# One transformer block on each of eight cores: an earlier first stage, biases as one tile, the last units by tokens

## The reference, cut

```python
xn = layernorm(x)                              # over 1024 channels
q, k, v = split(xn @ W_attn + b_attn)          # 16 heads of 64
att = (q @ k^T) / 8 / temperature + slope_h * (key - query)   # causal
y = softmax(att) @ v @ W_proj + b_proj
h = silu(xn @ (w_gate/127).T) * (xn @ (w_up/127).T)           # 3072 wide
out = x + y + h @ (w_down/127).T
```

## Time and profile before

| what | us |
|---|---|
| median of 3 runs, slowest core | 1230.04 (1229.83 to 1230.42) |
| the profiled execution, device time | 1233.72 |
| its span on core 0, the slowest | 1232.2 |
| spans of the other seven cores | 1224.6 to 1229.4 |
| TensorE busy | 1139.7 (92%) |
| VectorE / ScalarE / GpSimd busy | 588.8 / 528.7 / 239.5 |
| chain that ended last: TensorE's share | 84% |

### The profile page before, as it was taken

One profiled execution on the slowest core, in us unless ns is written; L12 is line 12 of the kernel. 1 busy time (PEld: TensorE's weight loads), 2 busy tenths in 40 slices (PEclk: granted clock), 3 DMA queues, 4 the chain that ended last, 5 costly groups with the idle time before them and its releaser, 6 DMA issues.

```text
span 1232.2 us, 24735 instructions; the slowest of 8 cores (1224.6 to 1232.2 us)
## 1 busy us (share of the span) xinstructions
PE 1139.7 (92%) x7874; PEld 574.5 (47%) x7874; DVE 588.8 (48%) x1194; ACT 528.7 (43%) x963; POOL 239.5 (19%) x292
## 2 busy tenths in 40 slices
PE   2899899999999999999999999999899689999996
PEld 1333345555555555555555555555454234444442
DVE  4442476666666666676566666667661100100000
ACT  0343335665666565565565655556575100000000
POOL 9000112222212222222222112122123300000000
PEclk9999899999999999999999999999999989999998
DMA  8229004322222332132312102122322441424220
GB/s 191 69 87 192 18 28 83 69 62 47 59 58 65 66 66 58 40 69 63 65 36 52 42 23 57 31 52 65 113 53 95 136 163 69 171 98 171 74 69 34
DMA packets 39724, 94.20 MB, mean 76 GB/s; under 512 B 5824, under 2 KB 26433, under 8 KB 38770
## 3 DMA queue, kind: packets, MB, share of 16 engines
q0 software_dynamic: 10352, 44.05, 16.9%
q1 hardware_dynamic: 28768, 48.45, 12.4%
q10 hardware_dynamic: 482, 0.12, 0.0%
HBM read 90.50 MB, written 27.26 MB: 96 GB/s over the span
## 4 chain that ended last, share of the span: by engine, by line
PE 84%; DVE 7%; issue 4%; POOL 2%; DMA 1%; ACT 1%; DVEq 0%; POOLq 0%; ACTq 0%; SPq 0%
PE ps_gu L701 24%; PE ps_dn L866 14%; PE ps_s L790 9%; PE ps_t L771 9%; PE ps_m L682 8%; PE ps_y L806 5%; PE ps_t L733 5%; PE ps_dn L853 4%; DVE cm L544 4%; DMA hb<-h_sc 1%; PE ps_m L819 1%; PE ps_t L775 1%; PE ps_s L793 1%; PE ps_t L737 1%; PE ps_dn L858 1%
## 5 line engine op out<-in xcount | busy, mean ns | idle before, releaser
L544 DVE TENSOR_REDUCE cm<-ps_s 128x1 f32<-128x512 f32 (+3 forms) x640 | 381.4, 608 | 223.9 <-PE ps_s L790 123.4
L650 ACT ACTIVATE pt<-ps_t 128x512 bf16<-128x512 f32 (+1 forms) x576 | 327.6, 576 | 214.3 <-PE ps_t L771 147.4
L701 PE MATMUL ps_gu<-xnT,wubuf 128*128 128x512 bf16 x768 | 264.0, 382 | 2.1 <-DVE hst L472 1.8
L701 PE MATMUL ps_gu<-xnT,wgbuf 128*128 128x512 bf16 x768 | 261.5, 380 | 1.2 <-ACT kst L593 1.2
L790 PE MATMUL ps_s<-kx,qx 67*128 67x512 bf16 (+3 forms) x640 | 219.3, 351 | 29.1 <-DVE cm L544 28.7
L771 PE MATMUL ps_t<-qx,kx 98*128 98x512 bf16 (+3 forms) x640 | 217.1, 349 | 0.6 <-ACT pt L650 0.6
L417 POOL TENSOR_SCALAR th_s<-th_s 128x512 f32<-128x512 f32 x96 | 59.3, 618 | 662.5 <-ACT th_s L601 662.5
L866 PE MATMUL ps_dn<-wdres,hb 128*128 128x512 bf16 x768 | 170.8, 383 | 13.9 <-DMA hb<-h_sc 13.9
L806 PEld LDWEIGHTS ps_y<-Vt,pt 128*128 128x128 bf16 x2176 | 126.5, 97 | 92.5 <-issue 1.3
L806 PE MATMUL ps_y<-Vt,pt 128*128 128x65 bf16 x2176 | 139.8, 193 | 0.0
L582 DVE SCALAR_TENSOR_TENSOR outsb<-ps_dn,xres 128x512 f32<-128x512 f32 x32 | 20.6, 686 | 226.9 <-PE ps_dn L866 226.9
(11 more groups left out here) (76 smaller groups left out, 799.7 us busy)
## 6 DMA issues: line engine op xcount, KB each, us to landing
h_sc<-hst SPq DMA_DIRECT2D x96, 128.0 KB, 1.7
hb<-h_sc SPq DMA_DIRECT2D x4, 3072.0 KB, 13.9
xstage<-xin SPq DMA_DIRECT2D x16, 512.0 KB, 4.7
xres<-xin POOLq DMA_DIRECT2D x16, 512.0 KB, 4.7
out<-outsb POOLq DMA_DIRECT2D x16, 512.0 KB, 3.0
wgbuf<-wg_r POOLq DMA_DIRECT2D x12, 512.0 KB, 6.9
wubuf<-wu_r POOLq DMA_DIRECT2D x12, 512.0 KB, 9.2
wd_sc<-wd_r POOLq DMA_DIRECT2D x12, 512.0 KB, 9.2
```

The costliest lines, as they stand in the source:

```text
L544: e.tensor_reduce(cm[:, c0:c0 + 1], ps_s[:, s % 2 * 512:s % 2 * 512 + w], AX.X, AluOpType.max, negate=True).then_inc(sem["v_mx"], 1)
L650: e.activation(pt[t % NPT][:, 0:w], ps_t[:, t % 2 * 512:t % 2 * 512 + w], AF.Exp).then_inc(sem["a_e"], 1)
L701: mm = e.matmul(ps_gu[:, r // 8 * 512:r // 8 * 512 + 512], w[:, w0:w0 + 128], xnT[:, dc * T + tb * 512:dc * T + tb * 512 + 512], start=(dc ...
```

## The change

- **First stage.** VectorE starts on x without waiting for constants: only TensorE waits for the identity (`l_id`), and VectorE waits for the other four (`l_const`) at i = 1, between tile 0's and tile 1's work. The matmul for the temperature moves to i = 3. GpSimd holds the weights back until the first two x tiles have landed, then issues the first half of the V weights, `wqk_b`, and the second half. V is made of the first column half alone for tiles 0 to 3 (`v_at`); then come q and k of block 0, then the second column half for tiles 0 to 3; from tile 4 on both halves follow each other.
- **Biases.** The rows L737 and L858, `onesb_s`, `bpj_b` and VectorE's work on them are gone. Since the weights of a softmax sum to one, the bias of V reaches the output as `b_v @ W_proj + b_proj`, the same for all tokens. TensorE makes this once before the output stage, in all 128 rows (16 matmuls of bf16 with `bv_b` broadcast and 2 of f32), ScalarE copies it to `bias_b`, and GpSimd adds it to each `xres` tile.
- **Last units by tokens.** Unit f >= 88 takes channels 22 and 23 of token block 0, then of block 1, and so on (`gu_of`). SyncE loads `hb0` after the store of unit 89.
- **Output.** ScalarE issues the stores of `out`; of the last tile the first half is finished before the second is begun, and each is stored alone.

```diff
+            return (f // 4, f % 4) if f < NF_ATT else (f // 8 * 2 + f % 2, f % 8 // 2)
...
+        v_at = {i: [(i - 1, 0)] for i in range(1, 5)}
+        v_at[4] += [(tt, 1) for tt in range(4)]
+        for i in range(5, NT + 1):
+            v_at[i] = [(i - 1, 0), (i - 1, 1)]
...
@@ block.sync
             for f in range(NF_ATT, NF):
                 store_h(f)
-            for tb in range(NTB):
+                if f == NF_ATT + 1:
+                    e.wait_ge(sem["s_h0"], 16 * HCN)
+                    e.wait_ge(sem["p_av"], len(tg))
+                    e.wait_ge(sem["p_yt"], 4 * NHP)
+                    e.dma_start(out=hb0[:, :], in_=h_sc[0, :, :]).then_inc(sem["l_hb0"], 16)
+                    e.dma_start(out=bpj_f[:, :], in_=bproj[:, :]).then_inc(sem["l_bp"], 16)
+            for tb in range(1, NTB):
@@ block.gpsimd
-            for d in range(4):
-                e.dma_start(out=wv_b[:, d * 2048:(d + 1) * 2048],
-                            in_=wv_r[:, d * 2048:(d + 1) * 2048]).then_inc(sem["l_wv"], 16)
-            cast_qk(0)
...
+            e.wait_ge(sem["l_x0"], 16)
+            e.wait_ge(sem["l_x1"], 16)
+            for half in range(2):
+                e.dma_start(out=wv_b[:, half * 4096:(half + 1) * 4096], in_=wv_r[half, :, :]).then_inc(
+                    sem[f"l_wv{half}"], 16)
+                if half == 0:
+                    cast_qk(0)
...
+                if tt >= 2:
+                    e.wait_ge(sem["v_out"], 2 * (tt - 1))
+                    e.dma_start(out=xres[tt % 2][:, :], in_=xin[tt * 128:(tt + 1) * 128, :]).then_inc(
                         sem[f"l_xr{tt % 2}"], 16)
+                if tt == 0:
+                    e.wait_ge(sem["a_b"], 2)
+                e.wait_ge(sem[f"l_xr{tt % 2}"], 16 * (tt // 2 + 1))
+                e.tensor_tensor(xres[tt % 2][:, :], xres[tt % 2][:, :], bias_b[:, :], AluOpType.add).then_inc(
+                    sem["g_xr"], 1)
@@ block.vector, gate_times_up and the first stage
-                if f >= 4:
+                if f >= NF_ATT + 4:
+                    e.wait_ge(sem[f"s_h{gu_of(f - 4)[1]}"], 16 * HCN)
+                elif f >= 4:
                     e.wait_ge(sem[f"s_h{f % 4}"], 16 * (f // 4))
...
+                if i == 1:
+                    e.wait_ge(sem["l_const"], 16 * 4)
@@ block.tensor
+                if i == 3:
+                    e.wait_ge(sem["v_t"], 3)
+                    e.wait_ge(sem["l_const"], 16 * 4)
...
+                    if i == 4 and x == 1:
+
+                        e.wait_ge(sem["a_xe"], 4)
                         e.wait_ge(sem["l_wq0"], 16)
                         e.wait_ge(sem["a_c"], 1)
+                        q_or_k(0, 0, ps_m, range(DC)).then_inc(sem["p_qk"], 1)
+                        q_or_k(0, 1, ps_y, range(DC)).then_inc(sem["p_qk"], 1)
+                        e.wait_ge(sem["l_wv1"], 16)
...
+            for half in range(2):
+                ps = ps_m if half else ps_y
+                for cc in range(DC):
+                    e.matmul(ps[:, :], bv_b[:, cc:cc + 1].broadcast_to([128, 128]),
+                             wpj_b[:, cc * C + half * 512:cc * C + half * 512 + 512], start=(cc == 0),
+                             stop=False)
+                e.matmul(ps[:, :], onesf_s[0:1, :], bpj_f[0:1, half * 512:half * 512 + 512], start=False,
+                         stop=True).then_inc(sem["p_b"], 1)
```

More of the change, by code:

```diff
@@ L580, in _ @@
                 for half in range(2):
+                    if tt == NT - 1 and half == 0:
+                        e.wait_ge(sem["p_dl"], 1)
+                    else:
+                        e.wait_ge(sem["p_d"], tt + 1)
                     bk = (tt % 2) * 2 + half
@@ L707, in gate_up @@
                         mm.then_inc(sem["p_u"], 1)
-            e.wait_ge(sem["l_const"], 16 * 7)
-            e.wait_ge(sem["v_t"], 3)
-            e.matmul(ps_m[:, 0:1], onesf_s[0:1, :], c11_s[0:1, :], start=True, stop=True).then_inc(sem["p_c"], 1)
+            e.wait_ge(sem["l_id"], 16)
             for i in range(NT + 2):
@@ L721, in _ @@
                     mm.then_inc(sem["p_xT"], 1)
-                if 1 <= i <= NT:
-                    tt = i - 1
+                if i == 3:
+                    e.wait_ge(sem["v_t"], 3)
+                    e.wait_ge(sem["l_const"], 16 * 4)
+                    e.matmul(ps_m[:, 0:1], onesf_s[0:1, :], c11_s[0:1, :], start=True, stop=True).then_inc(
+                        sem["p_c"], 1)
+                for x, (tt, half) in enumerate(v_at.get(i, [])):
+                    n = V0[i] + x
                     e.wait_ge(sem["a_xe"], tt + 1)
@@ new lines, in _ @@
+                    if n >= 2:
+                        e.wait_ge(sem["a_v"], n - 1)
+                    for dc in range(DC):
+                        mm = e.matmul(ps_t[:, n % 2 * 512:n % 2 * 512 + 512],
+                                      xnT[:, dc * T + tt * 128:dc * T + (tt + 1) * 128],
+                                      wv_b[:, half * 4096 + dc * 512:half * 4096 + dc * 512 + 512],
+                                      start=(dc == 0), stop=(dc == DC - 1))
+                    mm.then_inc(sem["p_v"], 1)
@@ L841, in _, with out_part @@
             e.wait_ge(sem["v_mx"], len(sg))
             e.wait_ge(sem["a_e"], len(tg))
-            e.wait_ge(sem["a_yt"], 4 * NHP)
-            e.wait_ge(sem["l_wp"], 16)
-            e.wait_ge(sem["v_bp"], 4)
+            def out_part(tt, kind, half, last):
+                tb, ts = divmod(tt, 4)
+                r0 = tt % 2 * 1024 + half * 512
+                if kind < DC:
+                    return e.matmul(ps_dn[:, r0:r0 + 512],
+                                    YT[:, kind * T + tt * 128:kind * T + (tt + 1) * 128],
+                                    wpj_b[:, kind * C + half * 512:kind * C + half * 512 + 512],
+                                    start=(kind == 0), stop=False)
+                hc = kind - DC
+                return e.matmul(ps_dn[:, r0:r0 + 512],
+                                hb[tb % 2][:, hc * 512 + ts * 128:hc * 512 + ts * 128 + 128],
+                                wdres[:, hc * 1024 + half * 512:hc * 1024 + half * 512 + 512],
+                                start=False, stop=last)
@@ L846, in _ @@
             for tt in range(NT):
                 tb, ts = divmod(tt, 4)
-                r0 = tt % 2 * 1024
                 if tt >= 2:
                     e.wait_ge(sem["v_out"], 2 * (tt - 1))
-                for cc in range(DC):
-                    for half in range(2):
-                        e.matmul(ps_dn[:, r0 + half * 512:r0 + half * 512 + 512],
-                                 YT[:, cc * T + tt * 128:cc * T + (tt + 1) * 128],
-                                 wpj_b[:, cc * C + half * 512:cc * C + half * 512 + 512],
-                                 start=(cc == 0), stop=False)
@@ L870, in _ @@
+                for kind in range(DC + HCN):
+                    if kind == DC and tt == 0:
+                        e.wait_ge(sem["l_wd"], 16 * HCP)
+                    if kind == DC and ts == 0:
+                        e.wait_ge(sem[f"l_hb{tb % 2}"], 16 * (tb // 2 + 1))
+                    for half in range(2):
+                        mm = out_part(tt, kind, half, kind == DC + HCN - 1)
                 mm.then_inc(sem["p_d"], 1)
```

184 lines of the change are left out of this document (82 added, 102 removed), and 2 rows, old and new, of the table SEMS.

## The result

The changed kernel runs in 1179.67 us (median of four runs, 1178.64 to 1180.64) against 1230.23 (1229.83 to 1231.42) for the kernel before: ratio 0.9579, 95% interval [0.9561, 0.9597]. Executions in which the cores of a die were granted a lower clock took 2 to 17% longer; all medians and ratios in this document leave them out.

The account below looks back on a forecast made before the run. TensorE was taken as the bound, busy 776.5 of 806.2 us in attention and 229.5 of 229.5 in output. First stage -19.3, seam -13.9, output -8.1, end -1.5 sum to -42.8 off 1230.04: 1187.2 us, range 1181 to 1199.

Parts of the forecast that it names:

- End: After the last matmul: one VectorE half instead of two, half the last store, GpSimd's late start; -1.5 us, 0 to -2.5.
- First stage, start: Up to tile 6's transposes: they begin at 52.1 us instead of 61.84, -9.7 us.
- Waits for the second half of the weights: First stage's start: TensorE waits some 5 us for that V weight half, taken as in at 40 us.
- at the very latest: First stage's start: tile 4 ready by 32 us even if memsets make tiles 0 to 4 each 2 us late.
- The memsets, set at 0: First stage's start: GpSimd's twelve memsets slow VectorE, hidden under TensorE's weights wait; 0, without that cover up to 4 us.
- Rival 4: First stage's start: constants land at 17.8 us and hold VectorE at tile 1; 1187 to 1190 us, chance 0.06.
- First stage, rest: From tile 6's transposes on: bias rows gone, 0.74 us per tile, -8.1; stop before tile 6 and slow groups gone, -1.5.
- Attention: Attention stage: plan left alone by the diff, change set at 0, between -3 and +3 us.
- Seam: Between last units and output: hb load hidden, bias tile added, tile 0 ends at 989.4 instead of 1003.3; -13.9 us.
- stall at unit 94: Last units: VectorE waits for stores behind the moved hb load; a 20 us load makes +5, 1192; chance 0.08.
- Output: Output stage: two bias matmuls less in 15 further tiles, 0.54 us each; -8.1 us.
- rival 3: Output stage: GpSimd's chain of xres load and addition sets the pace, 1230 us and more, slower than before; chance 0.01.

Follow-up runs that it names:

- the run of both edits: Changed kernel with q taken out of ps_m one token tile later and the second V weight half issued behind six more memsets and x tile 5: 1174.32 us, 0.9532.

## Why the prediction was wrong

**End: the step that failed.** I forecast -1.5 and measured -8.9 us. I followed the chain only to GpSimd's last issue at 1222.23. The span ends at 1232.2, and of the ten us between I priced only the store's bytes and "GpSimd's late start". The store had landed by 1225.2; the rest was GpSimd's drain, 6.757 us, a term that I had put at nothing, and the diff takes GpSimd out of the end. My bound of -2.5 had the same gap, so the range's low end had no room for it. With -8.9 in the term's place the sum is 1179.8 us. That it comes so close to 1179.67 is chance in part: the other terms were out by 3.0 us together, and the execution of before that I summed against lay 3.7 above its median.

**First stage, start: -9.7 forecast, -8.2 measured, by another mechanism.** The first V half (20 to 22 us forecast, 21.7 measured, 19.0 to 21.7 over the cores) was right. "Waits for the second half of the weights" was wrong on all eight cores: that half was in at 31.5 to 34.1 us, before TensorE asked for it, and the x tile was what came late. I had summed all bytes at one rate and given x its share first; beside the second half of the weights the tile took 12.0 to 14.9 us, without it 7.3 to 10.1. So tile 4, which I had bounded at 32 us "at the very latest" from VectorE's own work, was ready at 35.1 on core 3. The memsets, set at 0 under that wait, were then partly uncovered: `xn_st` takes 1.91 us in the chain above and 0.81 with no memset beside it, so 1.1 us at tile 4. The same shows ahead of the late tile: 2.31 and 2.15 us for tiles 0 and 1 on core 3, and SyncE issues tile 5's load only when tile 1 is normalised. What that cost was not measured. The Trainium skill (SBUF — State Buffer, Who interferes with whom) describes such a lock between the two engines, held for a whole instruction, and the rows agree. Rival 4 came true in small, too: the constants held VectorE until 12.1 to 12.8 us on six cores, not 17.8.

**First stage, rest: -9.6 forecast, -12.8 measured.** The rows give 0.85 per tile, not 0.74 (11 tiles: 1.2 us more). The slow groups behind tile 6's stop were 1.5 us, as forecast, and 0.2 more with the bias row between them. But the slowest core of before has them once more, behind its third stop:

```profile
113.64 2.76 PE ps_t L733 x8
...
116.93 2.33 PE ps_t L733 x8
```

That is another 1.7 us, at a granted clock of 0.74 from 113.0 to 119.6, and the slowest core of after has them behind neither of its two stops (16 matmuls in 3.61 us). The other seven of after do, once (5.30 us for 16 on core 5), so this part says which core was slowest and not what the change did. The median core needed 71.6 us for this stretch before and 60.6 after, 11.0 less: the 9.6 forecast and the 1.2 of the neighbours. For the start, it gained 10.4, from 61.8 to 51.4. Two stops stay, as forecast, and the run without them puts them at 7.2 us.

**Attention: 0 forecast, -2.6 measured.** The slowest core of before, 838.8 us, was the worst of its kernel, and the only one with a stretch at 0.50 behind attention's start. Core 0, then core 1, which took 834.8:

```profile
136.00:145.00 9.00, 7.86 (x25) 3.09 (x25) 4.83 (x10) 2.96 (x4) 1.26 (x2) 0.50 0.00 0
```

```profile
136.00:145.00 9.00, 6.71 (x41) 3.31 (x42) 6.84 (x15) 4.44 (x7) 1.77 (x2) 1.00 0.00 0
```

The others of before stand at 834.8 to 836.3, those of after at 832.1 to 836.2, where the 836.2 is again the core with the longest such stretch. In the run of both edits such a stretch went with 2 to 4 us between cores, so here it is the likely, not a tested, cause of what sets the slowest core apart. That the median core too fell, from 834.9 to 833.3, was not explained. All of it lies inside the -3 to +3 of the forecast.

**Seam: -13.9 forecast, -11.1 measured** (from the end of the last up matmuls to the end of tile 0: 30.7 before, 19.6 after). The mechanism held: `hb` was issued at 930.8 and in by 945.1, before the first matmul with it at 958.2, with no wait and no stall at unit 94. I had taken the end of the gates, 970.3, for that of the units, but the up matmuls ran to 972.6, so 2.3 us of what I took off were work that stays. The f32 matmuls are 1.05 us each where I took 0.87, above the 1 us that I had named as a sign; no row stood behind my upper bound of 1.9. (The 953.5 for unit 89's store should have been 952.9 by the rows; nothing hangs on it.) The chain after:

```profile
948.96 1.73 PE ps_y L882 x8
950.68 1.05 PE ps_y L885 x2
...
954.62 3.56 PE ps_dn L896 x16
958.18 10.36 PE ps_dn L901 x48
968.54 3.45 PE ps_dn L896 x16
971.99 10.36 PE ps_dn L901 x48
```

**Output: -8.1 forecast, -9.6 measured.** 3.45 + 10.36 = 13.81 us per tile instead of 14.45: the rows' neighbours again. GpSimd's addition is 2.34 us (2.3 forecast) and hidden: TensorE has no idle time in the stage, so rival 3 fails at its premise.

**The parts against the whole.** Singly, with the bias rows -22, the early load -16, GpSimd's drain -7.5, the last tile -1.2 and the bias tile +5.7 (948.96 to 954.62), the sum is -41. The rest of the 50.5, some 9 us, falls to the earlier start and the column halves. The first stage shows as much: 120.4 to 121.0 us without the bias rows, 109.7 to 113.6 in the changed kernel. The halves undone alone cost 8.6. How the 9 us divide between the start and the halves is not shown, since no run had the new start without the rest.

## What to carry to other kernels

Follow the chain to the span's end and not to the last visible instruction: what an engine does after its last wait, its drain above all, is on the path if that engine ends last, and here a change that only swaps who waits was worth 7.5 us. When work is cut from between others, take its price from a period with it and one without it, not from its own row. And a wait taken from the slowest core is worth only what the next wait there leaves: two of the runs moved attention's start by 3 to 6 us on some cores and the time not at all.

## What the runs showed of the hardware that was not expected

- GpSimd's drain at the program's end took 5.287 us behind a wait with an addition long done, 5.35 behind the end of an addition, and 6.757 where its last instruction was the issue of a store, each alike on eight cores; beginning with the issue of a load it took 7.2 to 8.2. ScalarE's took 0.008 us behind its own stores.
- Two bias matmuls between others cost more than their own time: the period shrinks by 0.85 us in the first stage and 0.64 to 0.65 in the output stage, where their own time was 0.64 and 0.54.
- The same attention instructions took 831.9 to 836.1 us on the cores of one run; the four cores at 835.8 and above had a stretch at 1.2 GHz behind attention's start.
- A wait of 8.9 us for weights was followed by 8 matmuls in 3.57 us, at a granted clock of 0.50, and after a stop of 1.84 us by 16 in 5.30, against 1.73 and 3.45 at the full clock.
- Small constants on the same DMA engines as 2.6 MB of weights held VectorE for 9.8 to 13.9 us where the weights were issued first, and for 0 to 2.5 us where they were held back until two x tiles were in.
- A tile of x of 512 KB took 12.0 to 14.9 us to land beside the second half of the weights and 7.3 to 10.1 without it.
